# Transformer decoder layer with 48 experts: two scatter chains, DRAM rows by partition, and four moves

## The reference

```python
x = _layernorm(x + attn(x, ...))      # complex-decay recurrence, gate, MLP of 1024
x = _layernorm(x + xattn(x, ctx, ctx, ...))  # causal attention, 16 heads of 16
x = _layernorm(x + ffn(x, ...))       # 48 experts, each takes its top 64 tokens
```

```python
vals, idx = jax.lax.top_k((xf @ Wr.T).T, cap)
w = jax.nn.softmax(vals, axis=-1)
h = gelu(einsum('ecd,esdm->ecsm', xf[idx], W1) + b1[:, None])
y = einsum('ecsm,esmk->ecsk', h, W2) + b2[:, None]
out = zeros_like(xf).at[idx.reshape(-1)].add((y.reshape(E, cap, D) * w[..., None]).reshape(-1, D))
```

## Time and profile before

| | |
|---|---|
| three runs | 811.88, 815.03, 816.0 us; median 815.03 |
| profiled execution | 816.48 us, span of the trace 814.7 |
| TensorE clock granted, mean | 0.884 |
| PE busy, VectorE, ScalarE, GpSimd | 612.5, 358.4, 274.5, 195.1 us |
| chain of waits, by engine | PE 49%, DMA 16%, DVE 15%, issue 9%, ACT 7%, POOL 3% |
| HBM read and written | 91.9 and 17.8 MB |

### The profile page before, as it was taken

The page is one execution under the profiler, slowest core; times in us unless marked ns, Lnnn a source line. Parts: engine busy times, 40 slices in busy tenths (PEclk is TensorE's granted clock), DMA queues, the critical chain, the costliest instruction groups (busy, mean ns, idle before and its releaser), DMA issues.

```text
span 814.7 us, 12126 instructions
## 1 busy us (share of the span) xinstructions
PE 612.5 (75%) x3942; PEld 351.0 (43%) x3942; DVE 358.4 (44%) x777; ACT 274.5 (34%) x458; POOL 195.1 (24%) x253
## 2 busy tenths in 40 slices
PE   3599999999467877787778788760089979789930
PEld 2458585847133445344534454340035535445520
DVE  3633533322564555455635564329823323223315
ACT  2141514141025463546354636510033322223304
POOL 1242221210051211021102111200032233335324
PEclk9899999999569899989998989965589999898965
DMA  6840000003410341134113334018159999994247
GB/s 229 299 162 1 0 0 0 25 27 108 138 40 1 113 140 45 40 116 135 38 46 114 109 114 179 1 53 338 84 176 372 408 387 326 315 378 88 35 98 231
DMA packets 53618, 112.25 MB, mean 138 GB/s; under 512 B 5920, under 2 KB 44496, under 8 KB 50512
## 3 DMA queue, kind: packets, MB, share of 16 engines
q1 hardware_dynamic: 48272, 105.06, 35.8%
q0 software_dynamic: 4608, 6.29, 4.1%
q10 hardware_dynamic: 704, 0.47, 0.2%
HBM read 91.88 MB, written 17.83 MB: 135 GB/s over the span
## 4 chain that ended last, share of the span: by engine, by line
PE 49%; DMA 16%; DVE 15%; issue 9%; ACT 7%; POOL 3%; SPq 1%; ACTq 0%; DVEq 0%; POOLq 0%
DMA sums<-row 9%; PE PS L1451 7%; PE PS L1442 7%; DMA sums<-wo_s,row 4%; DVE Mx L991 4%; PE PS L1730 4%; PE PS L1526 4%; PE PS L1610 3%; PE PS L1597 3%; PE PS L1567 3%; PE PS L1518 2%; PE PS L1413 2%; PE PS L1430 2%; PE PS L1563 2%; PE PS L1545 2%
## 5 line engine op out<-in xcount | busy, mean ns | idle before, releaser
L991 DVE TENSOR_REDUCE Mx<-PS 128x1 f32<-128x384 f32 (+3 forms) x176 | 107.3, 638 | 85.4 <-PE PS L1567 83.7
L1292 ACT ACTIVATE arena<-PS 128x512 f32<-128x512 f32 (+1 forms) x176 | 86.0, 565 | 87.6 <-PE PS L1597 87.6
L711 POOL TENSOR_SCALAR_AFFINE_SELECT arena<-arena 128x512 f32<-128x512 f32 x64 | 40.8, 638 | 217.9 <-ACT arena L1292 217.9
L1597 PE MATMUL PS<-arena 99*128 99x512 bf16 (+3 forms) x256 | 55.8, 307 | 26.3 <-ACT arena L1279 12.6
L1563 PE MATMUL PS<-causal,identb 128*128 128x128 bf16 (+2 forms) x176 | 45.8, 260 | 34.0 <-DVE Mx L991 24.7
L1567 PE MATMUL PS<-arena 96*128 96x128 bf16 (+3 forms) x256 | 68.1, 322 | 0.0
L1147 DVE TENSOR_TENSOR X<-PS,Y 128x512 f32<-128x512 f32 x48 | 31.4, 688 | 66.7 <-PE PS L1743 66.4
L1442 PE MATMUL PS<-arena 128*128 128x512 f32 x128 | 55.8, 593 | 1.6 <-issue 1.6
L1451 PE MATMUL PS<-arena 128*128 128x256 f32 x256 | 55.9, 379 | 0.0
L1359 ACT ACTIVATE X<-X 128x512 f32<-128x512 f32 x48 | 29.6, 632 | 71.3 <-DVE X L1147 68.1
L1610 PE MATMUL PS<-arena 128*32 128x128 f32 (+3 forms) x512 | 52.3, 481 | 1.0 <-POOL arena L711 0.9
(11 more groups left out here) (183 smaller groups left out, 997.6 us busy)
## 6 DMA issues: line engine op xcount, KB each, us to landing
ring_a<-experts SPq DMA_DIRECT2D x12, 2048.0 KB, 10.2
arena<-experts SPq DMA_DIRECT2D x12, 2048.0 KB, 10.3
arena<-pieces SPq DMA_DIRECT2D x192, 64.0 KB, 2.3
ring_a<-experts SPq DMA_DIRECT2D x12, 512.0 KB, 4.8
arena<-experts SPq DMA_DIRECT2D x12, 512.0 KB, 7.4
pieces<-arena SPq DMA_DIRECT2D x4, 768.0 KB, 3.7
pieces<-ring_a SPq DMA_DIRECT2D x4, 768.0 KB, 3.7
X<-x SPq DMA_DIRECT2D x4, 512.0 KB, 3.6
```

What stands on the lines that cost most here:

```text
L711: pool.affine_select(out=pb[j % 2][:, :, 0:P], in_=pb[j % 2][:, :, 0:P], compare_op=ALU.is_ge, fill=0.0, base=0, pattern=[[0, GH], [1, P]] ...
L991: dve.tensor_reduce(Mx[:, g % 2, i, heads[0]:heads[-1] + 1], bank((g * NSH + u) % 2)[:, 0:len(heads) * w] .rearrange("p (h n) -> p h n", h ...
L1292: act.activation(pb[j % 2][:, heads[0]:heads[-1] + 1, 0:w], bank(2 + n % 3)[:, 0:len(heads) * w] .rearrange("p (h n) -> p h n", h=len(heads)),
L1597: mm = pe.matmul(bank(2 + n % 3)[:, a * w:(a + 1) * w], KTs[0:SX, g * GH + h, j * P:(j + 1) * P], QTs[0:SX, g * GH + h, j * P:T], start=Tr ...
```

## The change

- **Scatters.** `sums` has four quarters of 2048 rows instead of two halves. Pairs 0 to 15 alternate between two chains: even pairs add into quarters 0 and 1, odd ones into 2 and 3 (`APART` = 16). Pairs 16 to 23 all go on chain 0. A scatter waits only for the one before it on its chain, `after_addition` is gone, and VectorE waits for the scatter six pairs back itself. GpSimd's loop over pairs is written out. Quarters 2 and 3 are loaded on chip (two loads of 2 MB into weight buffers that are free after pairs 17 and 18) and added together in four pieces behind the scaling of pairs 20 to 23 (`join`). The end adds three parts where it added two.
- **Rows by partition.** `x2_rows` and `sums` are ordered (p b t) instead of (b t p): what one partition holds of a batch is 4 KB in a row instead of four times 1 KB. Top-k's token numbers are turned into such rows by five more instructions; one more shifts the odd pairs by two quarters.
- **Group loads.** The head dimension of K and Q is reordered on the host so that a row of `pieces` has its four heads behind each other; a group is loaded by 6 DMAs, of 48, 32 and 16 partitions by 4 KB, instead of 12.
- **Moves.** The ones in KTs are written when the MLP is done, before `root(ln3, B-1)`. `project(1)` stands before `turn_2(0)`. The statistics and the norm of batch 0 stand before the phases. Zeros are written over three quarters, 6 MB instead of 2.

```diff
-K_PIECES = (0, 1, 2, 0, 1, 0)
-Q_PIECES = (0, 0, 0, 1, 1, 2)
-NRD = 2 * NPR
+K_RUNS = ((0, 1, 3), (0, 1, 2), (0, 1, 1))
+Q_RUNS = ((0, 0, 3), (1, 0, 2), (2, 0, 1))
+NRD = len(K_RUNS) + len(Q_RUNS)
+APART = 16
     x2_rows = nc.dram_tensor("x2_rows", (B * T, D), F32, kind="Internal").ap()
-    sums = nc.dram_tensor("sums", (2 * B * T, D), F32, kind="Internal").ap()
+    sums = nc.dram_tensor("sums", (4 * B * T, D), F32, kind="Internal").ap()
...
+        apart_sums = [slot[n][:, 0:B * TT * D].rearrange("p (a d) -> p a d", d=D)
+                      for n in (RING - 1, 0)]
...
-        SHIFTED, CHOSEN, TOPK = 36, 42, 47
+        SHIFTED, CHOSEN, TOPK = 36, 47, 53
+        def chain(p):
+
+            return (p % 2, p // 2) if p < APART else (0, p - APART // 2)
-        x2_v = x2_rows.rearrange("(b t p) d -> b p t d", p=P, b=B)
-        sums_v = sums.rearrange("(a b t p) d -> a b p t d", p=P, b=B, a=2)
+        x2_v = x2_rows.rearrange("(p b t) d -> b p t d", p=P, b=B)
+        sums_v = sums.rearrange("(a p b t) d -> a b p t d", p=P, b=B, a=4)
+        sums_all = sums.rearrange("(a p n) d -> a p n d", p=P, a=4)
...
-            sp.dma_start(sums[B * T:, :].rearrange("(a p) d -> p a d", p=P), wide(zrow[:], B * TT))\
-                .then_inc(zsum, 16)
+            for a in range(1, 4):
+                sp.dma_start(sums_all[a], wide(zrow[:], B * TT)).then_inc(zsum, 16)
...
-                rows_g = slice(GH * HD * (g % 2), GH * HD * (g % 2) + GH * HD)
-                for n, (dst, order) in enumerate(((KTs, K_PIECES), (QTs, Q_PIECES))):
-                    for r, c in enumerate(order):
-                        sp.dma_start(dst[HD * r:HD * r + HD, heads, :],
-                                     pieces[n, c, g // 2, rows_g, :]
-                                     .rearrange("(h d) t -> d h t", d=HD)).then_inc(kq_in[g].s, 16)
+                at = GH * (g % 2)
+                for n, (dst, runs) in enumerate(((KTs, K_RUNS), (QTs, Q_RUNS))):
+                    first = 0
+                    for c, step, count in runs:
+                        part = pieces[n, c:c + (count if step else 1), g // 2]\
+                            .rearrange("c (d h) t -> c d h t", d=HD)[:, :, at:at + GH, :]\
+                            .rearrange("c d h t -> c d (h t)")
+                        if not step:
+                            part = part.to_broadcast([count, HD, GH * T])
+                        sp.dma_start(dst[first:first + HD * count, heads, :]
+                                     .rearrange("p h t -> p (h t)"), part).then_inc(kq_in[g].s, 16)
+                        first += HD * count
...
-            sp.wait_ge(scattered, 16 * NP)
+            sp.wait_ge(scattered[1], 16 * APART // 2)
+            for n in range(2):
+                sp.wait_ge(y2m.s, y2m.now(NP - RING - 1 + n, 1))
+                sp.dma_start(apart_sums[n], sums_all[2 + n]).then_inc(apart_in, 16)
+            sp.wait_ge(scattered[0], 16 * (NP - APART // 2))
             for b in range(B):
                 sp.dma_start(X[:, b * TT:(b + 1) * TT, :], sums_v[0, b]).then_inc(fin_in[b], 16)
                 sp.dma_start(Y[:, b * TT:(b + 1) * TT, :], sums_v[1, b]).then_inc(fin_in[b], 16)
...
             pool.memset(Vb[:, :, :, HD:HD + 1], 1.0).then_inc(vset, 1)
+            pool.wait_ge(vset, 2)
+            pool.wait_ge(m2.s, m2.now(B - 1, 1))
+            for g in range(NG):
+                pool.memset(KTs[SK:SX, GH * g:GH * g + GH, :], 1.0).then_inc(ones, 1)
+            pool.wait_ge(ones, NG)
             root(ln3, rs3, B - 1, 1 + 2 * TT)
             pool.wait_ge(rs3.s, rs3.now(B - 1, 2))
...
-            pool.wait_ge(m2.s, m2.now(B - 1, 1))
-            for g in range(NG):
-                pool.memset(KTs[SK:SX, GH * g:GH * g + GH, :], 1.0).then_inc(ones, 1)
-            pool.wait_ge(ones, NG)
             with_bias(0)
...
 
                 pool.wait_ge(six.s, six.now(p, 1))
                 pool.sem_inc(pool_held, 1)
+                home, ahead = chain(p)
+                if ahead > 0:
+                    pool.wait_ge(scattered[home], 16 * ahead)
                 pool.wait_ge(yws.s, p + 3)
                 pool.sem_inc(pool_held, 1)
                 pool.indirect_dma_start(
-                    sums, bass.IndirectOffsetOnAxis(ap=sidx[u % RING], axis=0), ye[u % RING], None,
-                    compute_op=ALU.add).then_inc(scattered, 16)
-
-            def after_addition(p):
-
-                pool.wait_ge(scattered, (p + 1) * 16)
-                pool.sem_inc(added.s, 1)
+                    sums, bass.IndirectOffsetOnAxis(ap=sidx[u], axis=0), ye[u], None,
+                    compute_op=ALU.add).then_inc(scattered[home], 16)
 
             for p in range(RING):
                 gather(p, p)
             rows_of(0, 0)
-            with pool.Fori(0, NP // RING - 1) as r:
-                for u in range(RING):
-                    p = r * RING + u
-                    scatter(p, u)
-                    gather(p + RING, u, again=True)
-                    rows_of(p + 1, u + 1)
-                    after_addition(p)
-            for p in range(NP - RING, NP):
-                scatter(p, p)
+            for p in range(NP):
+                scatter(p, p % RING)
+                if p + RING < NP:
+                    gather(p + RING, p % RING, again=True)
                 if p + 1 < NP:
                     rows_of(p + 1, p + 1)
-                after_addition(p)
...
+            dve.wait_ge(x_in.s, x_in.now(0, 1))
+            statistics(ln1, X, 0, 0, 0)
             dve.wait_ge(consts, CONSTS)
             dve.wait_ge(w_vec, 16)
             link(dve.tensor_copy(ph, ph_i))
             link(dve.tensor_scalar(ph, ph, vec[:, V_FRQ:V_FRQ + 1], None, ALU.mult))
+            norm(ln1, rs1, X, lambda t: xn1[:, t, :], 0, 0, (xt1.s, xt1.before(0, 1)))
+            phase(0.0, rot[:, 0:C])
+            phase(0.25, rot[:, C:2 * C])
             dve.wait_ge(trig, 3)
...
+            col_of = far_i[lo, :]
+            then(dve.tensor_scalar(col_of, sel_i[lo, :], float(1 / P), 0.5 / P - 0.5, ALU.mult,
+                                   ALU.add))
+            then(dve.tensor_scalar(col_of, col_of, ROUND, None, ALU.add))
+            then(dve.tensor_scalar(col_of, col_of, ROUND, None, ALU.subtract))
+            then(dve.tensor_scalar(col_of, col_of, 1.0 - P * B * TT, None, ALU.mult))
+            then(dve.scalar_tensor_tensor(sel_i[lo, :], sel_i[lo, :], float(B * TT), col_of,
+                                          ALU.mult, ALU.add))
             dve.wait_ge(wexp, 1)
...
             then(dve.tensor_scalar(jcf, icf, off, None, ALU.add))
+            apart = jcf.rearrange("p (n a) -> p n a", a=2)[:, 0:APART // 2, 1]
+            then(dve.tensor_scalar(apart, apart, float(2 * B * T), None, ALU.add))
             then(dve.tensor_copy(jcol, jcf))
...
-            def weigh(p, u):
+            def weigh(p, u, free):
                 dve.wait_ge(y2m.s, y2m.now(p, 1))
-                dve.wait_ge(added.s, p + 1)
+                if free is not None:
+                    dve.wait_ge(*free)
                 dve.tensor_scalar(ye[u % RING], bank(5 + u % 2)[:, 0:D], wcol[:, bass.ds(p, 1)],
                                   None, ALU.mult).then_inc(yws.s, 1)
 
+            def join(b):
+
+                if b == 0:
+                    dve.wait_ge(apart_in, 32)
+                part = [m[:, b * TT:(b + 1) * TT, :] for m in apart_sums]
+                dve.tensor_tensor(part[0], part[0], part[1], ALU.add).then_inc(joined, 1)
+
...
-            with dve.Fori(0, NP // RING - 1) as r:
+            for u in range(RING):
+                second_half(u + 1)
+                hidden_bias(u + 1)
+                weigh(u, u, None)
+            with dve.Fori(1, NP // RING - 1) as r:
                 for u in range(RING):
                     p = r * RING + u
                     second_half(p + 1)
                     hidden_bias(p + 1)
-                    weigh(p, u)
+                    weigh(p, u, (scattered[u % 2], 16 * (3 * r + u // 2 - 2)))
             for u in range(RING):
                 p = NP - RING + u
                 if p + 1 < NP:
                     second_half(p + 1)
                     hidden_bias(p + 1)
-                weigh(p, u)
+                home, ahead = chain(p - RING)
+                weigh(p, u, (scattered[home], 16 * (ahead + 1)))
+                if u >= RING - B:
+                    join(u - RING + B)
 
             for b in range(B):
                 xb = X[:, b * TT:(b + 1) * TT, :]
                 dve.wait_ge(fin_in[b], 32)
                 dve.tensor_tensor(xb, xb, Y[:, b * TT:(b + 1) * TT, :], ALU.add).then_inc(fsum, 1)
-                dve.wait_ge(fsum, b + 1)
+                dve.wait_ge(fsum, 2 * b + 1)
+                if b == 0:
+                    dve.wait_ge(joined, B)
+                dve.tensor_tensor(xb, xb, apart_sums[0][:, b * TT:(b + 1) * TT, :], ALU.add)\
+                    .then_inc(fsum, 1)
```

(8 more changed lines are left out.)

14 lines of the change are left out of this document (7 added, 7 removed).

## The result

The changed kernel took **804.87 us** (median of 9 runs, 802.06 to 807.09), the kernel before 813.74 in the same comparison (9 runs): a ratio of **0.9884, interval 0.9856 to 0.9912**. The forecast was 793.1 with a range of 781 to 807. The time lies in the range and on the right side, but the gain is 9 us where 21.9 were summed. The profiled execution took 805.26, span 803.5, against 816.48 and 814.7. The one of the kernel before lies 2.7 us over its median and the changed one's 0.4 over its own, so the traces differ by 11.2 us where the medians differ by 8.9.

A forecast was written before the change was run, and what follows sets the result against it. The prediction took the experts' scatters, whose landing holds GpSimd's queue, as the first limit. Terms -21.6 + 0.8 + 3.1 - 4.2 - 2 + 2 = -21.9 took the profiled 816.48 to 794.6, 793.1 us on the median's footing; range 781 to 807.

The forecast's parts named there:

- 1.0 late. Three times, bounds 0 and 3: +2: Attention's three batch changes: the first group's loads land 1.0 us after they are wanted, adding 2 us in all.
- 13.0: Attention: time in us for a head group's loads, instead of 7.6, if only 3 and 2 engines share them.
- Hidden by 5 to 10 us: Experts' end: the two far loads of 2 MB finish before the first join behind pair 20's scaling; cost 0.
- quiet DMA: Pairs 16 to 23, one chain again: with little DMA traffic its scatters repeat every 3.8 to 4.8 us.
- The stall of 21.6: Experts: waiting for scatters to land costs 21.6 us between pairs 6 and 22; two chains remove it whole.
- The rival with one shared queue: Experts: both chains' scatters share one slow queue, so half or no gain, 804 to 814.7 us; chance 0.18.
- that of the weights: Experts: weight loads bind once pairs run at 6.69 us, up to 7 us back, 800 us; chance 0.05.
- The start of the attention, -2: PE's first shifted scores come earlier with the ones moved, despite slower first group loads: -2 us, bounds -2.9 and -0.8.
- the rival of sixteen engines: Attention: all sixteen engines share the group loads, giving about -9.7 us where the sum has 0; 783.4 us, chance 0.18.
- The prologue, -4.2: Before expand(0): earlier statistics and project(1) ahead of turn_2(0) make it begin 4.2 us sooner, 1.2 from the statistics.
- Top-k +0.8: Top-k: six more small instructions cost 1.4 us, partly covered by a wait of 0.58, net 0.8 us.
- the end +3.1: Final additions: two per tile group make VectorE the bound, 4.25 us a group; +3.1 us, bounds 2 and 4.

The follow-up runs named there:

- e1: Changed kernel with the 16 rows as outer dimension in the six loads of a head group, pieces inner: 785.18 us, ratio 0.9640.
- e2: Changed kernel with each head group loaded by twelve transfers of 16 rows from the new row order: 789.46 us, ratio 0.9690.
- e4: Changed kernel without the two far loads of 2 MB, so the output lacks the odd pairs' sums: 799.75 us, ratio 0.9841.
- e9: e1 with the far loads as eight of 512 KB, one every half pair from the end of pair 17: 783.95 us, ratio 0.9639.
- e3: Changed kernel with all scatters in one chain, without far loads, joins and third addition: 815.34 us, ratio 1.0024.
- e11: e3 with x2_rows and sums in their old row order, without the five token-number instructions: 813.76 us, ratio 0.9985.
- e12: e3 with the wait for the scatter's landing back behind the copy of the row numbers: 815.63 us, ratio 1.0015.
- e7: e1 with project(1) back behind turn_2(0): 791.49 us, ratio 0.9761.
- e8: e5 with the second copy of the sums added by GpSimd's DMA onto the on-chip sums, one VectorE addition less: 788.74 us, ratio 0.9717.
- e5: e1 with the far loads cut into eight of 512 KB, two after each of pairs 18 to 21: 787.46 us, ratio 0.9698.

## Why the prediction was wrong

Most mechanisms were right. Two terms of the sum failed, and they cost 12 of the 21.9 us.

- **"1.0 late. Three times, bounds 0 and 3: +2"** is the step that failed most. It measured +9.2, three times its upper bound. The assumption under it, a load shared out by the outermost cut, held (e1, e2). But it priced only the lateness, with 13.0 us for a group that took 14.85 at the change shown, and it left out what a wait does to the work behind it. The waits came to 5.4 us (1.83, 2.68 and 0.86) and the same matmuls ran 3.74 us longer. The bound of 3 had been made of one number, the lateness, and not of its consequences. The prediction did not ask either what else is loaded among the groups: a load of tokens issued there landed after 12.1 us and not 3.3. That both share the few engines, and that this lengthens the groups, is likely, but was not measured by itself.
- **"Hidden by 5 to 10 us"**, said of the far loads, is the second. It asked only whether VectorE would wait for them, and VectorE did not. But the text had also said that scatters are slow when the DMA is full, and for pairs 16 to 23, again one chain, it took "quiet DMA", while it was itself putting 4 MB there. The term was 0 and measured +4.9 us (e4: 3.8 of it goes with the loads, beside which the landing of pair 17 took 11.7 us and not 5.1, and e9 gets them back; the other 1.1 is there in e4 and e9 as well, 7.05 and 7.11 us where the kernel before has 5.93). Nor was DMA quiet for pair 16: its landing took 11.7 us in e4 too, behind the last weights. The chain made that up before its end.
- **The stall of 21.6** measured 23.2, with the pace of 6.65 us. The rival with one shared queue is out, and so is that of the weights: the pairs come at the pace that had been summed. By the medians some 19 of it are the second chain (e3, e11, e12).
- **The start of the attention, -2**, measured -2.06. The "13.0" stood for a first group that took 13.65; the rival of sixteen engines is out, and e1 shows what it would have given: 9.1 us at the start, of which 1.9 were lost up to the last store, 7.2 where the rival had 9.7.
- **The prologue, -4.2**, measured -3.18. The order of `project(1)` alone is worth 5.1 (e7). `mix(0)` happened to take 6.72 us, at half clock, in the profiled execution and 5.38 in that of the kernel before; without these 1.3 us of chance it is -4.5.
- **Top-k +0.8 and the end +3.1** measured +0.3 and +2.8. VectorE does bind the end.

Against the forecast, the two bad terms are +7.2 and +4.9, the others together -1.4: 10.7, which is 21.9 less 11.2.

## To carry to other kernels

When fewer, larger transfers replace many, look at what is outermost on both sides of each: here one `rearrange` of the source gave 17 to 20 us between medians (14.3 in the traces), with the same bytes and the same number of issues. Price a new wait with the work behind it, since PE can come back from it at its lower clock (0.50 behind the wait of 2.68 us here, but 1.00 behind that of 0.86), and ask of every transfer that is put into a quiet stretch who lives on its being quiet. A serial chain of small DMAs is such a tenant: with 4 MB going by it paid 11.7 us for a landing that took 5.1 without them, and its last link was as early as without them once they went by in steps and soon enough. Take the neighbour out before blaming it, though: the landing just ahead of that one took 11.7 us either way.

## What the runs showed of the hardware

- The granted clock after one and the same idle time differs from run to run. `mix(0)` comes after 2.85 us of idle PE in all profiled executions; its 16 matmuls took 6.72 us in the changed kernel and 3.69 in e1, with the same instructions up to there. The windows from 27 to 30, of the changed kernel and of e1:

```profile
27.00:30.00 3.00, 3.00 (x8) 0.50 0.46 148
```

```profile
27.00:30.00 3.00, 3.00 (x16) 1.00 0.47 151
```

  It took 3.69 us in seven of the fourteen profiled executions and 5.23 to 6.72 in the other seven. That shifts all that follows by up to 3 us, and two traces can only be compared once it is taken out; how much of the spread between the timed runs of one kernel comes from it (5 us over the nine of the changed kernel) is not shown. What decides it stayed open.
- With all engines at work, the group loads moved 195 GB/s at a DMA share of 1.01 (e1), while the kernel before had 405 GB/s at 1.02 with the weights, and the changed kernel's few engines 82 GB/s at 0.24. The same rows thus held an engine almost twice as long when all sixteen carried them. What this cost was not measured (only the first group is waited for), and its cause was not looked for.
- How long a scatter with addition (131 KB) takes to land went with what else the DMA carried: 11.7 us at a DMA share of 0.94 (e4, pair 16, 361 GB/s in the window), 5.1 at 0.35 (the next one).
- An adding DMA of 512 KB from DRAM onto the chip is no substitute for a plain one where its landing is waited for: 9.8 us for the first, where the plain load of the same rows needed 4.9 (e8, e5).
